# Last part of an eight-layer kernel: who adds the key and token projections, and who makes the norms

## The reference

```
h   = tanh(ctx @ Ws [1,key] + xn @ W [token,1] + b)      # every token with every key, width 128
rho = h @ w                                              # one score for each token and key
att = softmax(rho masked over the 77 keys)
w_s, b_s = tanh((att @ ctx) @ Wcw + bcw), tanh((att @ ctx) @ Wcb + bcb)
x = x + w_s * xn + b_s
# experts: softmax of xn @ wg, the largest of 8 wins, at most 1024 tokens each in token order
x = x + gate * (xn @ W[e].T + b[e])  where a place was left
```

## Time and profile before

| what | value |
|---|---|
| median of 3 runs | 3046.34 us (3044.14 to 3046.98) |
| span of the profiled execution | 3048.9 us |
| this part, first transfer to end | about 2190.8 to 3048.9 us |
| one turn once all steps run | 12.75 us |
| busy over the whole span | PE 90%, DVE 85%, ACT 78%, POOL 36% |

### The profile page before, as it was taken

The page is one execution under the profiler, slowest core; times in us unless marked ns, Lnnn a source line. Parts: engine busy times, 40 slices in busy tenths (PEclk is TensorE's granted clock), DMA queues, the critical chain, the costliest instruction groups (busy, mean ns, idle before and its releaser), DMA issues. The chain is left out here.

```text
span 3048.9 us, 79455 instructions
## 1 busy us (share of the span) xinstructions
...
## 2 busy tenths in 40 slices
...
DMA packets 177634, 91.21 MB, mean 30 GB/s; under 512 B 46339, under 2 KB 174021, under 8 KB 177251
## 3 DMA queue, kind: packets, MB, share of 16 engines
...
## 5 line engine op out<-in xcount | busy, mean ns | idle before, releaser
L2336 DVE TENSOR_TENSOR th<-tf 128x2048 f32<-128x2048 f32 (+1 forms) x256 | 574.2, 2244 | 6.6 <-ACT cg L2139 6.6
L2168 ACT ACTIVATE th<-th 128x2048 f32<-128x2048 f32 (+1 forms) x256 | 481.4, 1882 | 0.6 <-DVE th L2336 0.6
L652 ACT ACTIVATE probf<-probf,colf 128x128 f32<-128x128 f32 x1024 | 313.2, 393 | 0.0
L2116 POOL TENSOR_SCALAR colf<-colf 128x1 f32<-128x1 f32 x64 | 134.8, 2107 | 441.1 <-DVE colf L2317 441.1
L2230 PE MATMUL p_rho<-th,late_w_row 128*32 128x128 f32 x8064 | 277.1, 276 | 4.0 <-ACT th L2168 3.8
L2230 PEld LDWEIGHTS p_rho<-th,late_w_row 128*32 128x32 f32 x8064 | 208.4, 109 | 28.5 <-ACT th L2168 5.5
L1765 PE MATMUL acc<-xnT_all,wT 128*128 128x512 f32 x384 | 181.8, 626 | 29.5 <-DVE tmax L1957 13.2
L2179 ACT ACTIVATE tl<-tf 128x128 f32<-128x128 f32 x640 | 199.6, 391 | 0.0
L656 ACT COPY probTf<-fp 128x1024 f32<-128x1024 f32 x128 | 129.5, 1012 | 44.9 <-PE fp L800 44.9
L800 PE MATMUL fp<-ident,probf 128*128 128x128 f32 x1024 | 141.5, 283 | 24.9 <-ACT ygf L659 21.8
L1765 PEld LDWEIGHTS acc<-xnT_all,wT 128*128 128x128 f32 x384 | 73.6, 198 | 135.4 <-issue 83.4
...
## 6 DMA issues: line engine op xcount, KB each, us to landing
...
cxT<-in_ctxT SPq DMA_DIRECT2D x128, 38.5 KB, 1.9
...
```

What stands on the lines that cost most here:

```text
L652: last = nc.scalar.activation(scores, scores, ACT.Exp, bias=colf[s][:, 16 + HALF * hf + h:17 + HALF * hf + h])
L2116: nc.gpsimd.tensor_scalar(c[:, 8:9], c[:, 7:8], LN_EPS, None, ALU.add).then_inc(pool_done, POOL_L.did(f"{p}.eps", e))
L2168: nc.scalar.activation(b, b, ACT.Tanh).then_inc(act_done, ACT_L.did(f"t{c}.tanh", e))
L2336: nc.vector.tensor_tensor(th[i % NT][:, 0:shape[1], :], tf[s][:, CHUNK[n]:CHUNK[n + 1]].unsqueeze(2).to_broadcast(shape), tf[s][:, FEAT:FE ...
```

## The change

Only `part_3` and its tables change (two classes that nothing used are also deleted).

- Keys: VectorE adds 51 keys in three chunks of 17, and reads the features from PSUM (the bank p_x, of which there are now two) and only the keys from SBUF. GpSimd adds the other 26 in two chunks of 13 (s.sum0, s.sum1), both inputs from tf in SBUF. ScalarE puts five chunks through tanh (t0 to t2, u0, u1). The ten one-key tanhs, the identity products of TensorE and their tanh are gone.
- GpSimd also takes x3.norm, f3.norm and f3.taken, and makes the gated residual in two steps: x3.y = xn * w_s + b_s, then x3.x = x + x3.y. VectorE's x3.x and ScalarE's x3.shift are gone.
- f3.exp and f3.eq write to the bank p_f instead of SBUF, and f3.first and f3.pick read them there. tf takes the two gate columns along, so the copy to cg is gone; for that ctx is padded to 128 columns, with nine GpSimd memsets ahead of the part. Rings: x and ctx 9 instead of 6 deep, pick and taken 4 instead of 2.
- All four tables are new. No turn offset is above 6, as before.

```diff
-    CHUNK = (0, KT - 1, 2 * KT - 1, 3 * KT - 1, 4 * KT - 1)
...
+    CHUNK = (0, 17, 34, 51)
...
+    POOLED = (51, 64, KEYS)
...
-        p_rT, p_x, p_s, p_f = (ctx.enter_context(nc.psum_tensor(n, [128, BANK], F32)) for n in ("p_rT", "p_x", "p_s", "p_f"))
+        p_x = [ctx.enter_context(nc.psum_tensor(f"p_x{s}", [128, BANK], F32)) for s in range(2)]
...
+            def x3(e):
+                s, q = e % NX, e % NR
+                c = col[s]
+                yield from rstd("x3", e, c)
+                own("x3.rstd", e)
+                nc.gpsimd.tensor_scalar(xn[s][:], x[q][:], c[:, 6:7], c[:, 9:10], ALU.subtract, ALU.mult).then_inc(pool_done, POOL_L.did("x3.norm", e))
+                yield
+                act_gate = ACT_L.value("x3.gate", e)
+                pool.wait_ge(act_done, act_gate)
+                nc.gpsimd.tensor_scalar(xn[s][:], xn[s][:], c[:, 22:23], c[:, 23:24], ALU.mult, ALU.add).then_inc(pool_done, POOL_L.did("x3.y", e))
+                yield
+                own("x3.y", e)
+                nc.gpsimd.tensor_tensor(x[q][:], xn[s][:], x[q][:], ALU.add).then_inc(pool_done, POOL_L.did("x3.x", e))
...
+            def sums(e):
+                s = e % NX
+                for n in range(POOLS):
+                    i = POOLS * e + n
+                    pool.wait_ge(act_done, ACT_L.value("x3.proj", e))
+                    if i >= NP:
+                        pool.wait_ge(pe_done, PE_L.value(f"r.rhoP{(i - NP) % POOLS}", (i - NP) // POOLS))
+                    shape = [128, POOLED[n + 1] - POOLED[n], TOK]
+                    nc.gpsimd.tensor_tensor(tl[i % NP][:, 0:shape[1], :], tf[s][:, POOLED[n]:POOLED[n + 1]].unsqueeze(2).to_broadcast(shape),
+                                            tf[s][:, FEAT:FEAT + TOK].unsqueeze(1).to_broadcast(shape), ALU.add).then_inc(pool_done, POOL_L.did(f"s.sum{n}", e))
...
+                    own("f3.taken", e - 1)
+                    pool.wait_ge(dve_done, DVE_L.value("f3.pick", e - 1))
+                    if e >= 4:
+                        pool.wait_ge(pe_done, PE_L.value("f3.place", e - 4))
+                    nc.gpsimd.tensor_tensor(taken[n][:], taken[(e - 1) % 4][:], pick[(e - 1) % 4][:], ALU.add).then_inc(pool_done, POOL_L.did("f3.taken", e))
...
-                nc.scalar.copy(tf[s][:], p_x[:, 128:128 + KEYS + TOK])
-                nc.scalar.copy(cg[s][:], p_x[0:KEYS, 500:502]).then_inc(act_done, ACT_L.did("x3.proj", e))
+                nc.scalar.copy(tf[s][:], p_x[r][:, 128:128 + KEYS + TOK + 2]).then_inc(act_done, ACT_L.did("x3.proj", e))
...
-                nc.scalar.activation(x[e % NR][:], x[e % NR][:], ACT.Identity, bias=col[s][:, 23:24]).then_inc(act_done, ACT_L.did("x3.shift", e))
...
-                        last = nc.scalar.activation(tl[r][:, k, :], tf[s][:, FEAT:FEAT + TOK], ACT.Tanh, bias=tf[s][:, CHUNK[-1] + k:CHUNK[-1] + k + 1])
...
+                    act.wait_ge(pool_done, POOL_L.value(f"s.sum{n}", e))
+                    b = tl[(POOLS * e + n) % NP][:, 0:POOLED[n + 1] - POOLED[n], :]
+                    nc.scalar.activation(b, b, ACT.Tanh).then_inc(act_done, ACT_L.did(f"u{n}.tanh", e))
...
-                nc.scalar.activation(tl[r][:, TAIL - BY_PE:, :].rearrange("p k t -> p (k t)"), p_s[:], ACT.Tanh).then_inc(act_done, ACT_L.did("ts.tanh", e))
...
+                pe.wait_ge(pool_done, POOL_L.value("x3.norm", e))
+                if e >= 2:
+                    pe.wait_ge(act_done, ACT_L.value("x3.proj", e - 2))
+                    pe.wait_ge(dve_done, DVE_L.value(f"x3.sum{CHUNKS - 1}", e - 2))
...
-                nc.tensor.matmul(p_s[:], ident[:], tf[s][:, FEAT:FEAT + TOK].unsqueeze(1).to_broadcast(shape), start=True, stop=False)
-                nc.tensor.matmul(p_s[:], ident[:], tf[s][:, KEYS - BY_PE:KEYS].unsqueeze(2).to_broadcast(shape), start=False, stop=True).then_inc(pe_done, PE_L.did("s.sum", e))
...
                     nc.vector.tensor_tensor(th[i % NT][:, 0:shape[1], :], tf[s][:, CHUNK[n]:CHUNK[n + 1]].unsqueeze(2).to_broadcast(shape),
-                                            tf[s][:, FEAT:FEAT + TOK].unsqueeze(1).to_broadcast(shape), ALU.add).then_inc(dve_done, DVE_L.did(f"x3.sum{n}", e))
+                                            p_x[r][:, AT:AT + TOK].unsqueeze(1).to_broadcast(shape), ALU.add).then_inc(dve_done, DVE_L.did(f"x3.sum{n}", e))
...
-                nc.vector.scalar_tensor_tensor(x[q][:], xn[s][:], c[:, 22:23], x[q][:], ALU.mult, ALU.add).then_inc(dve_done, DVE_L.did("x3.x", e))
```

More of the change, by code:

```diff
@@ L187 @@
 PE_D = """
-    r.rho0@2 f3.kT@5 r.rhoL@2 f3.g@5 r.rho1@2 f3.y@5 r.rho2@2 f3.T@4 r.rho3@2 p.gate@3 f3.route@4 x3.T s.sum@1
-    r.rhoT@2 x3.proj p.PT@2 f3.place@4
+    f3.y@6 r.rho0@2 f3.T@5 r.rhoT@3 f3.route@5 r.rhoP0@2 r.rho1@2 f3.place@5 x3.T r.rhoP1@2 f3.kT@5 x3.proj f3.g@5
+    p.PT@3 r.rho2@2 p.gate@3
 """
 ACT_D = """
-    x3.rho@3 f3.exp@5 tb.tanh@2 ts.tanh@2 x3.exp@3 t1.tanh@2 x3.shift@5 f3.kT@5 t2.tanh@2 x3.proj@1 t3.tanh@2
-    ta.tanh@1 x3.PT@3 f3.xT@4 t0.tanh@1 x3.xT x3.gate@3
+    x3.xT x3.exp@3 f3.kT@5 t0.tanh@1 x3.PT@3 x3.proj t1.tanh@1 u1.tanh@1 x3.gate@3 x3.rho@2 f3.xT@4 u0.tanh f3.exp@4
@@ L194 @@
+    t2.tanh@1
 """
 DVE_D = """
-    f3.norm@5 x3.sum0@2 f3.out@6 x3.rden@4 x3.norm@1 x3.sum1@2 f3.nmax@5 x3.gb@4 x3.sum2@2 f3.rden@5 f3.eq@5 x3.nmax@3
-    f3.first@5 x3.x@4 f3.pick@5 f3.taken@5 f3.stats@4 x3.stats f3.keep@5 f3.aggr@4 x3.sum3@2 f3.xm@5 x3.aggr
+    f3.eq@6 f3.first@6 f3.pick@6 f3.stats@5 x3.nmax@4 f3.aggr@5 f3.keep@6 x3.sum1@2 x3.rden@4 f3.xm@6 x3.sum2@2
+    x3.gb@4 f3.out@6 x3.sum0@1 x3.stats f3.nmax@5 x3.aggr f3.rden@5
 """
 POOL_D = """
-    x3.rstd@1 f3.eps@4 f3.rstd@4 x3.eps
+    f3.taken@5 x3.eps x3.rstd x3.norm f3.eps@4 s.sum1@1 f3.rstd@4 f3.norm@4 s.sum0 x3.y@3 x3.x@3
@@ L2071, in part_3 @@
         colf = ring(2, "colf3", [128, 48])
-        pick = ring(2, "pick3", [128, MOE3], BF16)
-        taken = ring(2, "taken3", [128, MOE3], BF16)
+        pick = ring(4, "pick3", [128, MOE3], BF16)
+        taken = ring(4, "taken3", [128, MOE3], BF16)
         kept = ring(2, "kept3", [128, 3, MOE3], BF16)
```

233 lines of the change are left out of this document (70 added, 163 removed).

## The result

The changed kernel takes **3014.8 us** (3005.1 to 3020.6, four runs), the one before 3046.7 beside it (3044.1 to 3049.3, four runs): a ratio of 0.990 with a 95% interval of 0.988 to 0.991. It is faster, by 32 us where the forecast said 113, and outside the range. The profiled execution took 3016.5 us, with a span of 3014.4.

The account below looks back on a forecast made before the run. ScalarE never waits, with VectorE and TensorE nearly full, at 12.75 us a turn; the new walk, 10.67 to about 11.1, was taken as 10.9. Saving 1.85 us over 61 turns, 113 us, gives 2933 us, range 2905 to 2978.

Parts of the forecast that it names:

- the upper end: GpSimd's sum of 1664 columns: 3.38 us, a smaller row scaled by 3.25; 2.9 us was taken.
- rival 2: GpSimd is the bound, or u0 waits for its sum: 11.0 to 11.5 us a turn, 2939 to 2970 us; chance 0.17.
- f3.y late: TensorE's f3.y comes 0.35 us late, and VectorE's f3.out with it, as p.PT, 17 keys and p.gate stand ahead.
- f3.nmax to f3.keep: First stretch of the experts' walk on VectorE, with its waits, read from the drain: 1.74 us together.
- Head and drain: The part's start and end around its 61 steady turns: change counted as nothing, with 6 us either way.
- Rival 4: GpSimd is still shut out by VectorE's sums: 17.1 us a turn, time 3310 us, slower; chance 0.06.
- The two pairs of identity products: TensorE work that the change removes, priced at some 2 us of busy time a turn.
- the same walk: One turn of the experts' steps priced on VectorE, f3.nmax through sums, xm and f3.out to x3.stats: 10.67 us.
- Rival 3: Unseen waits (x3.T for the norm, x3.gate, or t2 before f3.kT) lose half the gain: 11.8 us, 2988 us; chance 0.05.
- rival 5: No change: losses from waits that the walk doesn't see just eat the gain; chance 0.02.
- the ring of the experts: Chain through VectorE, ScalarE and TensorE, from f3.nmax by f3.rden, f3.keep, xm and f3.out, expected to set the turn: 10.9 us.
- three signs that I had named for being wrong: GpSimd's sums lasting over 3.4 us, ScalarE waiting for tl, or TensorE's clock not at 1.00.

Follow-up runs that it names:

- run 5: The changed kernel with VectorE's three sums reading the features from SBUF instead of PSUM, so both inputs are in SBUF; 3336.3 us in one run.
- run 6: The changed kernel with the same instructions and only the four tables of order written anew; 2953.3 us, ratio 0.968 to the kernel before.
- run 10: The changed kernel with key chunks VectorE 16, 20, 16 and GpSimd 12, 13, and four tables written anew for them; 2942.3 us, ratio 0.964.
- run 2: The changed kernel with GpSimd's x3.norm adding the mean instead of subtracting it, its values changed; 2988.3 us, ratio 0.980 to the kernel before.

## Why the prediction was right in direction and wrong in size

*Right.* That a VectorE sum which reads PSUM leaves GpSimd free, and at no price: 2.41 us for 2176 columns, 2.33 from start to start as priced. GpSimd's sum, 2.98 us where I took 2.9 and the upper end was 3.38; the estimate from the Trainium skill (GPSIMD Engine Reference, Elementwise — side-by-side cycle accounting), 3.65, is too high for this form, and with it goes rival 2. f3.y late by 0.33, priced 0.35. f3.nmax to f3.keep 1.78, priced 1.74. Head and drain, 0.7 us where I took nothing with 6 either way. The clock, 1.00. The busy time of a turn: ScalarE 634.47 x 12.12 / 720 = 10.7 (10.6 forecast). GpSimd's is 10.1 too, but that is luck: the 10.1 of the forecast held 0.88 us of gaps. With its gaps GpSimd needs 12.12 - 1.58 = 10.5, as its two norms cost 0.8 each where I took 0.35. Rival 4 is out by GpSimd's rows and by run 5.

TensorE was under-priced: 665.61 x 12.12 / 720 = 11.2 us of busy time a turn, where I had written 10.1. The two pairs of identity products were worth 1.72 us and not 2 (from the first of them to r.rhoT's product behind them, 2619.34 to 2621.06 in the trace before). And the new cut of the keys costs TensorE more. Before, three chunks of 16 took 3 x 1.01, and the other 29 keys, in one piece with f3.kT, ran from 2610.44 to 2612.37, 1.93, less 0.15 for f3.kT: 4.81. Now two chunks of 17 take 2 x 1.21 and one of 13 takes 0.90. The other 13 and 17 follow one another directly, and such a pair takes 1.88 (run 6, r.rho1 and r.rhoP1, 2601.71 to 2603.59), less than 0.90 + 1.21: 5.20. I had counted the two cuts as equal. That makes 12.1 - 1.72 + 0.39 = 10.8. Four small products are longer from start to start than before, in another order: x3.T 0.26 (0.15), p.PT 0.26 (0.17), p.gate 0.32 (0.24), f3.route 0.32 (0.22), and f3.T is shorter, 0.16 (0.26). With them the sum is 11.1.

This doesn't set the changed kernel's turn, in which TensorE idles 0.9 us. It isn't a fixed floor either: under the tables of run 6 the same instructions are busy 11.0 us. But that too is above the forecast turn of 10.9, so neither of these orders could have reached it: run 6 comes to 11.21 with TensorE busy 98%, 61 x (11.2 - 10.9) = 18 us short of the forecast. Run 10, with the borders moved, has 10.88.

*Wrong: the step that failed.* "In the walk from f3.keep to xm TensorE has x3.T, 13 keys, f3.kT, the projections and f3.g to issue, some 3 us, against VectorE's one sum and one short instruction, 2.4 us and part of the wait for f3.place: this could be another 0.1 to 0.2 late." It was 0.94 late. The 3 us are right (3.08), the comparison isn't. Two things were missing:

- TensorE doesn't begin this list behind f3.place (its last piece ends at 2611.83) but at 2612.40, since its first entry, x3.T, waits for the norm on GpSimd: 0.58 us. Here the norm's price counts, 0.81 where I took 0.35; at 0.45 (run 2) x3.T waits 0.22.
- By the same rows, had it begun at once, xm would still have been 0.94 - 0.58 = 0.36 late, not 0.1 to 0.2.

So the sum, walked on VectorE with its waits, should have read: the same walk 10.85 (1.78 + 0.10 + 7.00 + 1.14 + 0.36 + 0.27 + 0.20; the two short ones cost 0.36, priced 0.2), f3.y 0.33, xm 0.94: 12.12.

Rival 3 had the mechanism by name, "x3.T for the norm"; the time, 3015, lies halfway between it (2988) and rival 5, no change (3046). I gave it 5% because "each of them has 0.5 us or more of slack in the order". That sentence had no working behind it. Behind x3.T's wait stand GpSimd's norm, then x3.aggr, x3.stats and x3.sum0 on VectorE, then f3.out, then f3.y, and f3.y stands in TensorE's queue behind x3.T of another example: going back from one norm one comes to the norm of the turn before, so it can have no slack that isn't the ring's. I had walked the ring of the experts on VectorE and taken the other engines' entries in it as hidden or as small additions, instead of walking through GpSimd. None of the three signs that I had named for being wrong came (GpSimd's sums 2.98 us, ScalarE waiting 0.5 us for tl in the whole stretch, the clock 1.00): they watched costs, and what failed was the order.

*What the change is worth.* Of the 1.85 us a turn that I forecast, 0.63 came at once, another 0.91 came by reordering alone (run 6), and the last 0.33, which makes 1.87 in all, came with another cut of the keys and tables written for it (run 10).
